# Self-attention block over 32x32 images: first block's chain and value weights reordered in the opening, second half of group 3 parted into heads and tails

## The reference

```python
y = ((xg - mu) * rsqrt(var + EPS)).reshape(B, C, H, W) * gamma + beta
qkv = einsum('bchw,dc->bdhw', y, w_qkv) + b_qkv
scores = einsum('bnc,bcm->bnm', q, k) * C ** -0.5
w = softmax(scores, axis=-1)
a = einsum('bnm,bmc->bnc', w, v)
out = einsum('bchw,dc->bdhw', a, w_out) + b_out
return x + out
```

## Time and profile before

| what | us |
|---|---|
| median of three runs | 134.29 (133.88 to 134.31) |
| the profiled execution, whole | 134.68 |
| its span, first to last instruction | 132.9 |
| TensorE busy | 126.7 (95%) |
| VectorE busy | 103.6 (78%) |
| GpSimd busy | 82.0 (62%) |
| ScalarE busy | 80.7 (61%) |
| DMA engines, between 10 and 30 us | share 0.01 and 0.00 |

### The profile page before, as it was taken

How to read it: one execution, slowest core, us unless ns; L and a number is a source line. 1 busy time by engine, 2 the same in 40 slices (tenths; PEclk the granted TensorE clock), 3 DMA queues, 4 the chain that set the end, 5 groups by cost and what they waited for, 6 DMA issues and landing times.

```text
span 132.9 us, 1913 instructions
## 1 busy us (share of the span) xinstructions
PE 126.7 (95%) x578; PEld 91.7 (69%) x578; DVE 103.6 (78%) x197; ACT 80.7 (61%) x140; POOL 82.0 (62%) x81
## 2 busy tenths in 40 slices
PE   6899989999999999999999999999998999999991
PEld 6787677777777566666765656776666778759890
DVE  0679886999999999769998785698886789667121
ACT  3066768776589656765963184579763895876000
POOL 5053175589448877973387678934999479843400
PEclk9999999999999999999999999999999999999999
DMA  4870000000039718993598759873899295952121
GB/s 152 273 284 2 0 5 0 0 2 0 0 70 205 165 41 192 205 207 109 118 209 195 194 115 201 199 199 72 189 210 223 59 202 117 200 158 79 39 83 40
DMA packets 6874, 16.65 MB, mean 125 GB/s; under 512 B 1872, under 2 KB 2128, under 8 KB 6864
## 3 DMA queue, kind: packets, MB, share of 16 engines
q1 hardware_dynamic: 6864, 16.53, 50.4%
HBM read 2.36 MB, written 2.10 MB: 34 GB/s over the span
## 4 chain that ended last, share of the span: by engine, by line
PE 55%; DVE 20%; POOL 12%; issue 5%; DMA 3%; ACT 2%; SPq 0%; DVEq 0%; POOLq 0%; ACTq 0%
PE mixed L927 16%; DVE scores L663 9%; DVE crossed L690 6%; PE scores L862 6%; PE scores L863 6%; PE scores L867 6%; POOL probs L367 5%; PE turned L881 3%; DMA xs<-in_x_dram 3%; POOL result L362 3%; POOL home_of_group L262 2%; PE turned L809 2%; POOL y_lo L343 2%; PE mixed L809 2%; DVE stats L578 2%
## 5 line engine op out<-in xcount | busy, mean ns | idle before, releaser
L367 POOL TENSOR_SCALAR probs<-probs,inv_sum 128x1024 f32<-128x1024 f32 x32 | 36.0, 1125 | 29.9 <-DVE inv_sum L668 29.7
L663 DVE TENSOR_SCALAR_CACHE_REDUCE scores<-scores,key_bias 128x1024 f32<-128x1024 f32 x31 | 39.9, 1287 | 8.6 <-PE scores L867 8.4
L462 ACT ACTIVATE probs<-scores,neg_max 128x1024 f32<-128x1024 f32 x32 | 35.7, 1117 | 17.4 <-DVE scores L663 16.6
L862 PE MATMUL scores<-y_hi,z_hi 128*128 128x512 f32 x62 | 33.3, 537 | 0.1
L690 DVE STREAM_TRANSPOSE crossed<-probs 128x1024 f32<-128x1024 f32 x24 | 29.8, 1242 | 1.5 <-POOL probs L367 1.4
L927 PE MATMUL mixed<-crossed,v 128*128 128x512 f32 x64 | 30.3, 593 | 0.0
L863 PE MATMUL scores<-y_lo,z_hi 128*128 128x512 f32 x62 | 24.4, 394 | 0.0
L867 PE MATMUL scores<-y_hi,z_lo 128*128 128x512 f32 x62 | 19.3, 392 | 0.0
L927 PEld LDWEIGHTS mixed<-crossed,v 128*128 128x128 f32 x64 | 11.6, 190 | 8.3 <-issue 7.2
L862 PEld LDWEIGHTS scores<-y_hi,z_hi 128*128 128x128 f32 x62 | 11.7, 188 | 7.9 <-issue 4.9
L863 PEld LDWEIGHTS scores<-y_lo,z_hi 128*128 128x128 f32 x62 | 11.7, 189 | 6.4 <-issue 4.8
(11 more groups left out here) (179 smaller groups left out, 212.9 us busy)
## 6 DMA issues: line engine op xcount, KB each, us to landing
crossed<-crossed SPq DMA_DIRECT2D x92, 128.0 KB, 2.4
out_dram<-result SPq DMA_DIRECT2D x7, 256.0 KB, 2.4
xs<-in_x_dram SPq DMA_DIRECT2D x4, 256.0 KB, 3.5
xs<-in_x_dram SPq DMA_DIRECT2D x2, 512.0 KB, 6.3
ws<-in_weights_dram SPq DMA_DIRECT2D x1, 256.0 KB, 3.7
out_dram<-result SPq DMA_DIRECT2D x2, 128.0 KB, 1.9
vecs<-in_vectors_dram SPq DMA_DIRECT2D x1, 3.0 KB, 3.4
```

The lines of the kernel that those rows point to most:

```text
L367: pool.tensor_scalar(probs[:, i % RING, :], probs[:, i % RING, :], inv_sum[:, i:i + 1], 1.0, ALU.mult, ALU.mult).then_inc(s_probs, 1)
L462: act.activation(probs[:, i % RING, :], scores[:, i % 2, :], ACT.Exp, bias=neg_max[:, i:i + 1], scale=-1.0, accum_out=row_sum[:, i:i + 1]) ...
L663: dve.tensor_scalar(scores[:, i % 2, :], scores[:, i % 2, :], key_bias[:, b % 2, i:i + 1], None, ALU.subtract, ALU.min, accum_out=neg_max[ ...
L862: pe.matmul(to[h], z_hi[:, b % 2, query], y_hi[:, b % 2, halves[h]], start=True, stop=False)
```

## The change

Four things are moved in the opening. (1) On VectorE the z tail goes behind the closing subtraction of block 0's maximum, whose key bias now waits for the values on TensorE and not for ScalarE's copy of them; that copy goes behind the first exponential. (2) The first reciprocal goes ahead of block 1's maximum. (3) The product of value and output weights goes up, ahead of the first group variances, into another bank, and its copy into the place behind that of the turned weights. (4) The first value tile is made while TensorE waits for the first piece of z, in place of one of two warming matmuls.

For group 3, pairs 2 and 3 (tiles 4 to 7) are parted: ScalarE copies a value head in turn 17 and both pairs' heads at the end of turn 19; VectorE subtracts for the value tail at the end of turn 17 and for pair 2's tail in turn 20, behind the flip and ahead of the reciprocal; GpSimd makes pair 3's tail in turn 21, ahead of its normalisation. `mix` takes 3, 1, 2 and 2 tiles in the four turns. There is new memory for heads and values; the tails lie in the home, as with the other parted pairs.

```diff
+    EARLY_PARTED = {2: "vector", 3: "gpsimd"}
-        for k, tiles in enumerate((2, 2, 2, 2) if group == 5 else (3, 2, 1, 2) if group % 2 else (1, 2, 3, 2)):
+        for k, tiles in enumerate((2, 2, 2, 2) if group == 5 else (3, 1, 2, 2) if group == 3 else (3, 2, 1, 2) if group % 2 else (1, 2, 3, 2)):
...
+        def early_tail(engine, k):
+
+            engine.wait_ge(s_early_heads, k - 1)
+            engine.tensor_tensor(pair_of_tiles(flat(tails_6), k), pair_of_tiles(crossed[:, HOME[3], :], k),
+                                 squares_by_query(early_heads[:, k - 2, :]).bitcast(fp32),
+                                 ALU.subtract).then_inc(s_early_tails[EARLY_PARTED[k]], 1)
...
+                    if BLOCKS * b + i == 21:
+                        early_tail(pool, 3)
...
+            act.wait_ge(s_value_weights, 1)
+            act.activation(wv_out[:, 0:C], turned[:, 0, 0:C], ACT.Copy).then_inc(s_setup, 1)
             act.wait_ge(s_folded, 1)
...
+            act.wait_ge(s_folded, 2)
+            act.activation(wv_out[:, C:C + 1], setup[:, SET_U:SET_U + 1], ACT.Copy, scale=SCALE).then_inc(s_setup, 1)
             act.wait_ge(s_z0, 1)
-            act.wait_ge(s_setup, 1)
+            act.wait_ge(s_setup, 2)
...
-            act.wait_ge(s_folded, 2)
-            act.activation(wv_out[:, 0:C], setup[:, SET_V:SET_V + C], ACT.Copy).then_inc(s_setup, 1)
-            act.activation(wv_out[:, C:C + 1], setup[:, SET_U:SET_U + 1], ACT.Copy, scale=SCALE).then_inc(s_setup, 1)
...
+            exponentials(0, 0)
+            act.wait_ge(s_key_bias, 1)
             first_values(V0, turned[:, 1, :])
-            exponentials(0, 0)
...
+                    if BLOCKS * b + i == 17:
+                        act.wait_ge(s_v, 6)
+                        act.activation(early_v_hi[:, :, :], v[:, 1, KT // 2:KT, :], ACT.Copy).then_inc(s_early_v_hi, 1)
+                    if BLOCKS * b + i == 19:
+                        act.wait_ge(s_swapped[1], swaps(3))
+                        for k in EARLY_PARTED:
+                            act.activation(squares_by_query(early_heads[:, k - 2, :]),
+                                           pair_of_tiles(crossed[:, HOME[3], :], k), ACT.Copy).then_inc(s_early_heads, 1)
...
-                    first_z_tail(1, turned[:, 0, FIRST:HALF], FIRST, HALF)
                     dve.wait_ge(s_setup, 5)
                     first_key_biases(V0, turned[:, 1, :])
                     dve.wait_ge(s_key_bias, 1)
                     dve.wait_ge(s_first_max, 1)
                     dve.tensor_scalar(neg_max[:, 0:1], first_max[:, :], key_bias[:, 0, 0:1], key_bias[:, 0, 0:1],
                                       ALU.subtract, ALU.add).then_inc(s_max, 1)
+                    first_z_tail(1, turned[:, 0, FIRST:HALF], FIRST, HALF)
...
+            inverse_sum(0, 0)
             maximum(0, 1)
-            inverse_sum(0, 0)
...
+                    if BLOCKS * b + i == 20:
+                        early_tail(dve, 2)
                     if i == 0 and b > 0:
                         projection_vectors(b, V2, mixed[:, 1, :])
...
+                    if BLOCKS * b + i == 17:
+                        dve.wait_ge(s_v, 6)
+                        dve.wait_ge(s_early_v_hi, 1)
+                        dve.tensor_tensor(early_v_lo[:, :, :], v[:, 1, KT // 2:KT, :], early_v_hi[:, :, :].bitcast(fp32),
+                                          ALU.subtract).then_inc(s_early_v_lo, 1)
...
+                    if group == 3 and k // 2 in EARLY_PARTED:
+                        pe.wait_ge(s_early_v_lo, 1)
+                        pe.wait_ge(s_early_tails[EARLY_PARTED[k // 2]], 1)
+                        head = early_heads[:, k // 2 - 2, :].rearrange("p (g v u c) -> p v u g c", g=SQ, v=2,
+                                                                       u=QB)[:, k % 2, :, :, :]
+                        tail = tile_by_query(flat(tails_6), k)
+                        pe.matmul(bank, early_v_hi[:, k - KT // 2, :], head, start=False, stop=False)
+                        pe.matmul(bank, early_v_hi[:, k - KT // 2, :], tail, start=False, stop=False)
+                        mm = pe.matmul(bank, early_v_lo[:, k - KT // 2, :], head, start=False, stop=final)
...
             pe.transpose(setup[:, SET_W + C:SET_W + 2 * C], WK_T, ident[:, :]).then_inc(s_w_turned, 1)
+            pe.matmul(turned[:, 0, 0:C], WV, WOUT_T, start=True, stop=True).then_inc(s_value_weights, 1)
             group_variances(0, 1, mixed[:, 0, :])
...
-            pe.matmul(setup[:, SET_V:SET_V + C], WV, WOUT_T, start=True, stop=True)
...
-            keep_warm(2)
+            pe.wait_ge(s_setup, 3)
+            value_tile(0, 0, turned[:, 1, :], 0)
+            keep_warm(1)
...
-            pe.wait_ge(s_setup, 3)
-            values(0, V0, turned[:, 1, :]).then_inc(s_v0, 1)
+            values(0, V0, turned[:, 1, :], done=1).then_inc(s_v0, 1)
```

More of the change, by code:

```diff
@@ L109, in attention_kernel @@
         v_hi, v_lo = sb("v_hi", [128, KT, C], fp32r), sb("v_lo", [128, KT, C], fp32r)
+        early_v_hi, early_v_lo = sb("early_v_hi", [128, KT // 2, C], fp32r), sb("early_v_lo", [128, KT // 2, C], fp32r)
+        early_heads = sb("heads_of_group_3", [128, 2, N], fp32r)
         mid_v_hi, mid_v_lo = sb("mid_v_hi", [128, KT, C], fp32r), sb("mid_v_lo", [128, KT, C], fp32r)
@@ L134, in attention_kernel @@
         last_banks = [scores[:, 0, 0:QUARTER], mixed[:, 1, 0:QUARTER]]
-        SET_W, SET_V, SET_OUT, SET_U, SET_S, SET_G, SET_Z = 0, 256, 384, 385, 386, 512, 640
+        SET_W, SET_OUT, SET_U, SET_S, SET_G, SET_Z = 0, 384, 385, 386, 512, 640
         centred, first_z = z_full[:, 0:FIRST], z_full[:, FIRST:2 * FIRST]
@@ L154, in attention_kernel @@
         s_wqk = sem("turned_weights_copied")
+        s_value_weights = sem("value_weights_multiplied")
         s_folded = sem("folds_done")
@@ L193, in attention_kernel @@
         s_diagonal = {"scalar": sem("diagonal_by_scalar_copied"), "gpsimd": sem("diagonal_by_gpsimd_copied")}
+        s_early_v_hi = sem("early_v_head_ready")
+        s_early_v_lo = sem("early_v_tail_ready")
+        s_early_heads = sem("heads_of_group_3_ready")
+        s_early_tails = {"vector": sem("group_3_tails_by_vector_ready"), "gpsimd": sem("group_3_tails_by_gpsimd_ready")}
         s_mid_v_hi = sem("mid_v_head_ready")
@@ L743, in first_key_biases @@
             def first_key_biases(job, bank):
-                dve.wait_ge(s_v, V_NO[job] + 1)
+                if job == V0:
+                    dve.wait_ge(s_v0, 1)
+                else:
+                    dve.wait_ge(s_v, V_NO[job] + 1)
                 key_biases(0, job, bank)
@@ L804, in group_variances, with values, value_tile @@
                           start=True, stop=True).then_inc(s_gvar, 1)
-            def values(b, job, bank):
+            def values(b, job, bank, done=0):
                 lo, hi = V_TILES[job]
-                for t in range(lo, hi):
-                    mm = pe.matmul(bank[:, (t - lo) * VW:(t - lo) * VW + C + 1], y[:, b % 2, t * 128:(t + 1) * 128],
-                                   wv_out[:, 0:C + 1], start=True, stop=True)
-                return mm
+                for t in range(lo + done, hi):
+                    mm = value_tile(b, t, bank, t - lo)
+                return mm
+            def value_tile(b, t, bank, place):
+                return pe.matmul(bank[:, place * VW:place * VW + C + 1], y[:, b % 2, t * 128:(t + 1) * 128],
+                                 wv_out[:, 0:C + 1], start=True, stop=True)
             def projection(b, job, bank):
@@ L908, in mix @@
                     first, final = k == 0, k == KT - 1
-                    if (group, k // 2) in MID_NUMBER:
+                    if group == 3 and k // 2 in EARLY_PARTED:
[7 more added lines that the diff above has]
+                        mm = pe.matmul(bank, early_v_lo[:, k - KT // 2, :], head, start=False, stop=final)
+                    elif (group, k // 2) in MID_NUMBER:
                         n = MID_NUMBER[group, k // 2]
@@ L1014, in _ @@
                     if b == 0 and i == 0:
-                        pe.wait_ge(s_key_bias, 1)
+                        pe.wait_ge(s_v, 1)
                     if not swapped(BLOCKS * b + i):
```

## The result

The changed kernel takes 135.43 us (median of 7 runs, 135.03 to 135.85), the kernel before 134.29 in the same comparison: ratio 1.0092, 95% interval 1.0075 to 1.0109, so +1.2 us, slower (+1.14 us by the two medians, +1.24 by the ratio). The forecast was 135.4. The profiled execution took 135.43 us, its span is 133.5. VectorE's busy time rose from 103.6 to 107.1 us, GpSimd's from 82.0 to 84.8, and TensorE's fell by 0.2, to 126.5.

A forecast was written before the change was run, and what follows sets the result against it. TensorE looked like the bound until 102 us, GpSimd right behind it, so GpSimd delays count in full. -0.33 (opening) + 1.4 (GpSimd loop) + 0.1 (block 17 tail) = +1.17, giving 135.4 us; 8-in-10 range 133.7 to 136.2.

The forecast's parts named there:

- the opening: First blocks, one serial chain: the reordering was to save 0.33 us in the end, between 0.1 and 0.55.
- inv 22: Reciprocal of block 22 on VectorE: behind pair 2's tail it comes at 85.2 us; it ran at 84.41 before.
- norm 22: Normalisation of block 22 on GpSimd: start moves from 85.19 to about 86.3 us, +1.1; without contention +0.1.
- The collision at turn 20: VectorE's tail of pair 2 beside GpSimd's z subtraction: GpSimd practically stands still, z ends near 86.2 us, +1.1.
- the second rival: No contention: GpSimd's z in block 20 runs at full speed, +0.45 - 0.33 = +0.1, 134.4 us; chance 0.19.
- z at 2.2 us: Sign in the later profile: GpSimd's z of batch 3's first half takes about 2.2 us in place of 1.29.
- TensorE's waits: About 1 us ahead of group 3's last two tiles, and longer than 0.47 us ahead of group 4's last pair.
- The value tail of turn 17: VectorE, block 17: fits 0.73 us idle before the maximum at 74.36; cost taken as 0.1 us, bounds 0 and 0.4.
- ScalarE's two head copies: After block 21's exponential: two copies of 1.05 us each, just covered by 1.97 us of ScalarE idle time.
- GpSimd's 2.4 us and the loop: Block 21: pair 3's 2.41 us tail makes block 23's normalisation +1.4 us; block 24's follows, nothing absorbs it.
- TensorE's 0.64 us: Group 3: four parted tiles at 0.70 us in place of 0.86 save 0.64 us on TensorE at best.
- TensorE is the bound: Rival: the tails hide, block 23's normalisation starts by about 88.4 us; total between 133.3 and 133.9 us; chance 0.21.

The follow-up runs named there:

- opening_only: The changed kernel without all edits for group 3, so only the opening's edits remain: 133.99 us, ratio 0.9970 to the kernel before.
- pair3_only: The changed kernel with only pair 3 parted (GpSimd's tail in turn 21), no VectorE tail in turn 20: 133.97 us, ratio 0.9991 to the kernel before.
- pair2_only: The changed kernel with only pair 2 parted (VectorE's tail in turn 20), no added GpSimd work: 135.49 us, ratio 1.0091 to the kernel before.
- z_filled: The changed kernel with GpSimd filling z's tail for the last image's first half with zeros instead of subtracting: 134.50 us, ratio 1.0014 to the kernel before.
- tail2_behind_inv: The changed kernel with VectorE's tail of pair 2 behind the reciprocal of block 22 instead of ahead: 135.54 us, ratio 1.0091 to the kernel before.

## Why the prediction was right, point by point

Times in the changed kernel, forecast (the working's times less the opening's 0.33) against measured:

| step | forecast | measured |
|---|---|---|
| maximum of block 4 | 22.84 | 22.85 |
| GpSimd's z beside VectorE's tail, length | 2.2 | 1.27 |
| VectorE's tail of pair 2, length | 1.2 | 2.23 |
| inv 22 | 84.9 | 85.96 |
| norm 22 | 86.0 | 86.21 |
| norm 23 | 89.5 | 89.66 |
| norm 24 | 92.6 | 92.81 |
| group 4's last pair on TensorE | 103.5 | 103.51 |
| total | +1.17 | +1.24 (ratio), +1.14 (medians) |

- **The opening: right in size, with one term mis-sized, and the close fit is partly luck.** -0.33 forecast, -0.32 at block 4's maximum in this profile, -0.4 by opening_only, with an interval of -0.8 to -0.05. Two things make it up. From the start of the variances' evacuation (`var_eps`, L602 in the kernel before) to block 4's maximum, all twelve profiles with the new opening take 15.85 to 15.88 us and the two with the old one 16.32 and 16.33: 0.46 gained. Ahead of that stands the value-weight product, taken at 0.1 between bounds of 0 and 0.3. In this profile the variances' matmul starts at 6.67, 0.38 us behind the end of its input, in place of 0.06, and the evacuation follows 0.22 later than it would. That leaves 0.24; the other 0.08 is that the first group means were that much earlier in this execution. In other executions the cost is anything from 0 to 0.7 us, beyond the forecast's bound, because the variances' matmul stands in TensorE's queue behind the transposes of the weights and now the product too. When the weights arrive late, all of them wait, as in the profile of opening_only, whose block 4 maximum (23.09) is only 0.08 us earlier than before. The transposes stood there in the kernel before as well, but in neither profile with the old opening were the weights late, so how much of the larger cost is the product's is open. The first transpose in opening_only:

```profile
6.43 0.33 PE L992 MATMUL scores<-ident,ws 128*128 128x128 f32 x1 [0.60 <-DMA ws<-in_weights_dram]
```

- **The collision at turn 20: its price right, its direction wrong.** The step "z ends near 86.2 and norm 22 starts at about 86.3" took VectorE for the one that comes first. GpSimd was first by 0.12 us. The other order stood among the arguments against the second rival, with norm 22 late through inv 22 and 1.5 us in the end; that is what happened. Either way one full instruction stands in the path of norm 22, and the two have nearly one length (1.27 and 1.22 us), hence the small difference in the sum. That the sum held with the order wrong is luck: the forecast's price was for the order that did not come. The place that the forecast named to look at, z at 2.2 us, would have told a reader that there was no contention; the sign of it was on the other engine.
- **TensorE's waits: half wrong.** The forecast had about 1 us ahead of the last two tiles of group 3. It is 1.64 us ahead of the two before them, for VectorE's late tail, and nothing ahead of the last. Ahead of group 4's last pair the wait did grow, from 0.47 to 0.53.
- **The value tail of turn 17: collides, and is absorbed.** Issued at 73.25, beside norm 19 (72.92, 1.13 us), it takes 1.33 us, and y behind norm 19 takes 1.62 in place of about 1.2. So the earlier trace rows did not tell enough: a gap of 0.73 us is of no use if the neighbour holds the way. Counted from norm 19, the maximum at 74.51 is 0.53 late; at block 21's exponential (78.61, before 78.85) 0.14 of it is left, and 0.12 at norm 22 of pair3_only. The forecast took 0.1 with a bound of 0.4.
- **ScalarE's two head copies: right.** By the rows they needed 2.10 us of a gap of 1.97; they ran from 79.71 to 81.71 and z's head followed at 81.66.
- **GpSimd's 2.4 us and the loop: right.** Counted from norm 19, pair 3 alone delays norm 23 by 0.37 us, pair 2 alone by 1.31 and both by 1.64 (forecast 1.5), with norm 24 3.1 to 3.2 us behind norm 23 in every kernel. Of the 1.66 at norm 24, 1.45 are left at norm 28.
- **TensorE's 0.64 us: not seen in any total, and in part in the traces.** Norm 25 follows norm 24 by 3.46 to 3.51 us in every kernel with pair 3 parted, by 3.61 or 3.62 where group 3 is left alone, by 3.83 in pair2_only, where it waits 0.33 us for its reciprocal. So in that stage TensorE's shorter work does count, but it only wins back a part of what the tails have cost. Pair3_only is level with opening_only within the intervals.
- The rival "TensorE is the bound" fell, as did "no contention"; z_filled, where there is none, measured +0.14%, 0.2 us, against the +0.1 us forecast for that case.

## What to carry to other kernels

Before giving idle time on one of VectorE and GpSimd more work, list what the other runs at that moment: here two subtractions over on-chip memory were serial on this pair, and moving one in its queue only changed which engine's instruction grew. Idle time inside a loop between engines can hold work but does not absorb lateness: a gap of 2.1 us took 2.4 us of work for 0.25 us, while the lateness of norm 22 went through every gap to norm 24. And to compare two traces, count from an event ahead of the change: they ran up to 1 us apart here, more than most effects. And after the change look for instructions of a known form that have grown, since this stall leaves no idle bracket.

## What the runs showed of the hardware

- VectorE's subtraction with both inputs in SBUF and a GpSimd instruction that reads SBUF excluded each other wherever they met, in both orders: 2.23 and 2.24 us for a tail of 1.2 behind GpSimd's z, 2.14 behind its residual, 1.33 for a 512-column tail behind norm 19; 2.11 for norm 22 behind the tail. A VectorE subtraction of 512 columns with one input in PSUM takes 0.68 (`last_turned_tail`). Beside a fill by GpSimd the tail took 1.18. The Trainium skill (SBUF — State Buffer, Who interferes with whom) says that a VectorE instruction with two SBUF inputs contends with a GpSimd instruction that reads SBUF and not with one that only writes it, that this is an exclusive lock, and that the order of issue decides who waits. The numbers agree: the fill did not hold up the tail, the stalls are as long as the rest of the other's instruction, and either engine was the one held up.
- An engine that already waited came ahead of the other's next instruction: in tail2_behind_inv VectorE's tail ran between z and norm 22, though norm 22 had its input for 0.7 us; in turn 17 the value tail ran between norm 19 and y in the same way.
- VectorE's transposes did not hold GpSimd up: its 2.39 us tail at 86.01 in pair3_only ran beside the flip at 86.07 (1.25 us, as elsewhere) at the length it has alone.
